# A selective scan and feed-forward block: four of sixteen u*B on ScalarE, C spread by transposes, ten C products on GpSimd

## The chip, the cores and the metric

The kernel runs on one core of a Trainium2 chip. A core has TensorE (matmuls), VectorE, ScalarE, GpSimd and SyncE (DMA queue); they run programs of their own and meet at semaphores. The metric is the device time of one execution, in microseconds.

## What is computed

The input is 16 sequences of 1024 tokens with 256 channels. First comes a selective scan with 16 states for each channel, then a normalisation, a gated feed-forward part with integer weights (hidden size 768), and a second normalisation.

```python
xz = einsum('btd,pd->btp', x, W_xproj)             # 64 rank, 16 B, 16 C
dt = softplus(einsum('btr,dr->btd', xz[..., :64], W_dt) + b_dt)
dA = exp(dt[..., None] * -exp(A_log))              # decay, per channel and state
dBx = dt[..., None] * B[:, :, None, :] * x[..., None]
h = dA_t * h + dBx_t;  y = sum_s h[..., s] * C[..., s]   # for each token
z = layernorm(x + y + Dp * x)
out = layernorm(z + (silu(z @ gate.T) * (z @ up.T)) @ down.T)
```

## The kernel before

The 16384 tokens are cut into 32 chunks of T = 512; two chunks make a sequence (par 0 and 1). Channels lie on the 128 partitions in DH = 2 halves q, tokens along the free dimension. All arithmetic on these tiles is f32, but for the gate and up matmuls (f16 in two parts).

For each chunk and state s, in this order: ScalarE makes the decay `exp(dt * a)` of each half into PSUM, in the one buffer `p_da` (L490); GpSimd makes `ub` = u * B_s (L388), where `u` = dt * x (L381) and B_s was spread over the partitions by a DMA through DRAM (`b_bc`); VectorE scans each half (L620) into `h`, which has eight slots; a product with C_s follows, in place, by GpSimd for the states of `POOL_STATES` (L398, C spread by DMA as `c_bc`) and by VectorE for the others (L629). For the latter TensorE spreads C_s into `p_c` by one bf16 matmul with a selector (L792), on three bf16 parts of the rows of C that `rest` and `third_part` (L594, L599) and three casts on ScalarE (L464, L468, L469) make. TensorE turns the products back to tokens on partitions and sums them over the states in `p_y` (L807). In chunks with par 0 ScalarE copies the last column as `h_carry` (L485), which the scans of the next chunk start from.

The rest of a chunk runs beside the scans of the next two: transposes and projections of the chunk ahead (`x_transposed`, `project`, `project_dt`, softplus in three ScalarE passes with a table load, `dt_of` L604), the first normalisation of the chunk behind (`stats1`, `mean1`, `norm_inputs`, a `pow` and a product on GpSimd L405 and L408, `norm1` L501), `x1_high` and `x1_low` (L506, L653), six tiles of gate and up matmuls (L831), `tanh` (L510), `silu` (L659), `hidden` (L665), and for the chunk two behind the down matmuls (L842), `residual` (L672), `stats2` and `norm2` (L518).

Each engine's order is written out by a loop over the 16 slots of a step (`step`), each with two or three zones; in slot s VectorE scans state s. The table `AT` gives the slot and zone of every other job. Ordinary u*B are made four slots ahead (`UB_AHEAD`), decays one ahead (`DA_AHEAD`), C products one behind (`C_LAG`, `POOL_LAG`), the sums two or three behind (`SUM_LAG`). An engine that waits holds up all that stands behind in its program:

```python
def decay(c, s, par, q):
    wait(act, s_dt, c + 1)
    wait(act, s_scan, 2 * units(c, s) - 2 + q - 1)   # scan of half q of the state before
def scan(c, s, par, batch, q):
    wait(dve, s_da, 2 * units(c, s) - 1 + q)
    if q == 0:
        wait(dve, s_ub, units(c, s))
```

Steps 0 and 1 are written out, a hardware loop runs pairs of steps, and the last steps are written out again; steps 32 and 33 hold only the normalisations and the feed-forward part of the last chunks.

Of the kernel before, what the change touches and what calls it, by code (L numbers as in the profile page):

```python
# [5 lines left out]
P = 128  # L6
# [7 lines left out]
T = 512  # L14
# [5 lines left out]
POOL_STATES = (1, 2, 4, 8, 9, 10, 11, 12)  # L20
# [7 lines left out]
SUM_LAG = {True: 3, False: 2}  # L28
# [19 lines left out]
B_GROUP = 4  # L48
UB_SLOTS = 8
# [3 lines left out]
def mamba_ffn_block(nc, x, w_xproj, w_dt, b_dt, a_log, d_skip, w_gate, w_up, w_down, out):  # L53
# [13 lines left out]

    assert N % B_GROUP == N % UB_SLOTS == N % H_SLOTS == 0

# [7 lines left out]
    with ExitStack() as ctx:  # L77
# [11 lines left out]
        selector = sb("selector", [P, N, P], BF16)  # L89
# [7 lines left out]
        wt_proj = sb("wt_proj", [P, DH, P], F32)  # L97
# [91 lines left out]
        s_b = [sem(f"s_b{k}") for k in range(N // B_GROUP)]  # L189
# [94 lines left out]
        def _(sp):  # L284
# [19 lines left out]
            def store(c):  # L304
                wait(sp, s_out_ready, c + 2)
# [30 lines left out]
            for k in range(N // B_GROUP):  # L336
# [27 lines left out]
        def _(pool):  # L364

            nc.gpsimd.memset(ident[:, :], 0.0).then_inc(s_fill, 1)
            nc.gpsimd.memset(selector[:, :, :], 0.0).then_inc(s_fill, 1)
            nc.gpsimd.memset(neg_half[:, :, :], -0.5)
            pool.wait_ge(s_fill, 2)
# [537 lines left out]
```

## Time and profile before

| | |
|---|---|
| median of 3 runs | 2120.16 us (2118.89 to 2121.01) |
| profiled execution, its time | 2119.75 us |
| its span, first to last instruction | 2118.0 us |
| mean granted TensorE clock | 0.928 of full |
| VectorE, GpSimd busy | 94%, 91% |
| TensorE, ScalarE busy | 74%, 62% |
| DMA | 239.9 MB, 113 GB/s |

PE stands for matmuls on TensorE, PEld for its weight loads, DVE for VectorE, ACT for ScalarE, POOL for GpSimd. A line such as L620 is a line of the kernel. Busy time is an average over the whole span, so the repeated part, the start and the tail have to be read apart.

### The profile page before, as it was taken

The numbers are of one execution on the slowest core, as the hardware profiler recorded it, in microseconds if no ns is written. First come the engines' busy times: TensorE is split into PE (matmuls) and PEld (weight loads), VectorE is DVE, ScalarE is ACT, GpSimd is POOL, SyncE is SP. The second block draws the span as 40 slices with busy tenths as digits, with TensorE's granted clock in tenths as the row PEclk, the third lists the DMA queues.
The fourth block names the chain that finished last, engine by engine and source line by source line (L and its number), as shares of the span: only waits on it lengthen the run. The fifth ranks groups of instructions, "written<-read, shape, count | busy, mean of one in ns | idle before, by whom it ended". The sixth has DMA issues, their size and how long they took to land.

```text
span 2118.0 us, 30230 instructions
## 1 busy us (share of the span) xinstructions
PE 1558.5 (74%) x8621; PEld 1140.7 (54%) x8744; DVE 1985.9 (94%) x2443; ACT 1303.6 (62%) x2157; POOL 1926.8 (91%) x877
## 2 busy tenths in 40 slices
PE   4677778777778777777777777777777877777775
PEld 1545555455555555555555555555555555555553
DVE  5799999999999999999999999999999999999982
ACT  4566666566666656666666666656666656666442
POOL 6999999999999999999999999999999999999950
PEclk6789999999999999999999999999999999999997
DMA  6332433223433322443322443422443422343200
GB/s 219 111 119 86 141 118 137 102 91 112 140 135 120 117 83 104 140 140 115 125 90 89 140 140 115 140 90 76 138 140 115 140 92 86 126 140 107 79 11 20
DMA packets 93455, 239.90 MB, mean 113 GB/s; under 512 B 8593, under 2 KB 42994, under 8 KB 77042
## 3 DMA queue, kind: packets, MB, share of 16 engines
q1 hardware_dynamic: 93426, 239.55, 32.5%
q8 instruction: 13, 0.21, 0.0%
q14 instruction: 16, 0.13, 0.0%
HBM read 220.65 MB, written 18.87 MB: 113 GB/s over the span
## 4 chain that ended last, share of the span: by engine, by line
issue 30%; POOL 28%; DVE 26%; PE 8%; ACT 6%; DVEq 2%; POOLq 1%; another core or an unknown queue 0%; ACTq 0%
POOL ub L388 16%; DVE h L620 10%; POOL h L398 8%; DVE h L629 6%; PE p_y L807 3%; DVE hid L665 2%; DVE silu_g L659 2%; ACT p_da L490 2%; DVE stats L635 2%; PE p_m L831 2%; DVEq L224 1%; PE p_o L842 1%; PE p_m L821 1%; POOL rstd L405 1%; DVE mean_var L639 1%
## 5 line engine op out<-in xcount | busy, mean ns | idle before, releaser
L388 POOL TENSOR_TENSOR ub<-u,b_bc 128x1024 f32<-128x1024 f32 x512 | 1203.9, 2372 | 0.1
L490 ACT ACTIVATE p_da<-dt,neg_a 128x512 f32<-128x512 f32 x1024 | 697.2, 687 | 426.1 <-DVE h L620 422.0
L620 DVE TENSOR_TENSOR_SCAN h<-p_da,h_carry,ub 128x512 f32<-128x512 f32 x512 | 641.5, 1271 | 2.2 <-ACT p_da L490 0.6
L398 POOL TENSOR_TENSOR h<-h,c_bc 128x1024 f32<-128x1024 f32 x256 | 606.8, 2371 | 33.5 <-ACT h_carry L485 32.8
L620 DVE TENSOR_TENSOR_SCAN h<-p_da,ub 128x512 f32<-128x512 f32 x512 | 610.1, 1212 | 8.1 <-ACT p_da L490 6.4
L807 PE MATMUL p_y<-ident,h 128*128 128x128 f32 x4096 | 572.2, 293 | 60.8 <-POOL h L398 59.6
L807 PEld LDWEIGHTS p_y<-ident,h 128*128 128x128 f32 x4096 | 518.8, 152 | 121.6 <-POOL h L398 81.9
L842 PE MATMUL p_o<-wt_down,hid 128*128 128x256 f32 x1536 | 353.7, 380 | 4.1 <-DVE hid L665 1.8
L842 PEld LDWEIGHTS p_o<-wt_down,hid 128*128 128x128 f32 x1536 | 287.6, 191 | 55.3 <-issue 13.9
L629 DVE TENSOR_TENSOR h<-h,p_c 128x1024 f32<-128x1024 f32 x256 | 306.1, 1196 | 9.8 <-PE p_c L792 5.2
L510 ACT ACTIVATE tanh_g<-p_m 128x512 f32<-128x512 f32 x192 | 114.7, 597 | 263.4 <-PE p_m L831 263.4
L831 PE MATMUL p_m<-x_t,wt_up 128*128 128x512 f16 x768 | 199.5, 382 | 80.5 <-DVE hid L665 78.6
L792 PE MATMUL p_c<-bc_parts,selector 128*128 128x512 bf16 x133 | 58.8, 442 | 268.4 <-DVE h L629 268.4
L831 PE MATMUL p_m<-x_t,wt_gate 128*128 128x512 f16 x768 | 199.7, 383 | 61.6 <-DVE x_t L653 55.1
L792 PEld LDWEIGHTS p_c<-bc_parts,selector 128*128 128x128 bf16 x256 | 26.8, 105 | 310.9 <-DVE h L629 208.4
L831 PEld LDWEIGHTS p_m<-x_t,wt_up 128*128 128x128 f16 x768 | 63.9, 98 | 207.7 <-DVE hid L665 149.9
L405 POOL TENSOR_TENSOR rstd<-var_eps,neg_half 128x8 f32<-128x8 f32 x33 | 54.0, 1638 | 130.3 <-DVE neg_mean L649 130.3
L659 DVE SCALAR_TENSOR_TENSOR silu_g<-tanh_g,p_m 128x512 f32<-128x512 f32 x192 | 127.9, 666 | 8.8 <-ACT tanh_g L510 8.8
L831 PEld LDWEIGHTS p_m<-x_t,wt_gate 128*128 128x128 f16 x768 | 64.4, 98 | 131.8 <-DVE x_t L653 62.8
L665 DVE SCALAR_TENSOR_TENSOR hid<-p_m,silu_g 128x512 f32<-128x512 f32 x192 | 128.1, 667 | 1.2 <-DVE silu_g L659 0.5
L381 POOL TENSOR_TENSOR u<-dt,x_t 128x1024 f32<-128x1024 f32 x32 | 76.4, 2388 | 18.1 <-DVE dt L604 18.1
L785 PE MATMUL p_m<-rank_t,wt_dt 65*128 65x512 f32 x128 | 67.9, 656 | 29.3 <-DVE bc_parts L599 29.3
(72 smaller groups left out, 1289.3 us busy)
## 6 DMA issues: line engine op xcount, KB each, us to landing
b_bc<-bc_rows_dram SPq DMA_DIRECT2D x128, 1024.0 KB, 4.7
c_bc<-bc_rows_dram SPq DMA_DIRECT2D x256, 256.0 KB, 6.5
x_in<-in_L_attn_x SPq DMA_DIRECT2D x32, 512.0 KB, 7.2
out_x<-res_n SPq DMA_DIRECT2D x32, 512.0 KB, 3.3
bc_rows_dram<-bc_rows SPq DMA_DIRECT2D x32, 64.0 KB, 2.3
hid<-in_L_ffn_w_gate SPq DMA_DIRECT2D x1, 768.0 KB, 4.9
hid<-in_L_ffn_w_up SPq DMA_DIRECT2D x1, 768.0 KB, 6.7
res<-in_L_ffn_w_down SPq DMA_DIRECT2D x1, 384.0 KB, 7.1
```

Source lines behind the costliest of these rows:

```text
L388: nc.gpsimd.tensor_tensor(ub[:, s % UB_SLOTS, :, :], u[:, par, :, :], b_bc[:, s:s + 1, :].broadcast_to([P, DH, T]), ALU.mult).then_inc(s_u ...
L398: nc.gpsimd.tensor_tensor(h[:, s % H_SLOTS, :, :], h[:, s % H_SLOTS, :, :], c_bc[:, i:i + 1, :].broadcast_to([P, DH, T]), ALU.mult).then_i ...
L490: nc.scalar.activation(p_da[:, q, :], dt[:, par, q, :], ACT.Exp, scale=neg_a[:, q, s:s + 1]).then_inc(s_da, 1)
L510: nc.scalar.activation(tanh_g[:, :], p_m[:, 0, :], ACT.Tanh, scale=0.5 / (QUANT * X1_SCALE)).then_inc(s_tanh, 1)
L620: nc.vector.tensor_tensor_scan(h[:, s % H_SLOTS, q, :], p_da[:, q, :], ub[:, s % UB_SLOTS, q, :], initial, ALU.mult, ALU.add).then_inc(s_s ...
L629: nc.vector.tensor_tensor(h[:, s % H_SLOTS, :, :], h[:, s % H_SLOTS, :, :], p_c[:, :, :].broadcast_to([P, DH, T]), ALU.mult).then_inc(s_hc ...
L659: nc.vector.scalar_tensor_tensor(silu_g[:, :], tanh_g[:, :], 1.0, p_m[:, 0, :], ALU.add, ALU.mult).then_inc(s_silu, 1)
L665: nc.vector.scalar_tensor_tensor(hid[:, j, :], p_m[:, 1, :], 1.0 / (2.0 * QUANT * QUANT * X1_SCALE * X1_SCALE), silu_g[:, :], ALU.mult, AL ...
L792: nc.tensor.matmul(p_c[:, 0, :], selector[:, s, :], bc_parts[:, par, :], start=True, stop=True).then_inc(s_c_ps, 1)
L807: ins = nc.tensor.matmul(p_y_tok[:, k, q * P:(q + 1) * P], h[:, s % H_SLOTS, q, k * P:(k + 1) * P], ident[:, :], start=False, stop=(s == S ...
L831: ins = nc.tensor.matmul(p_m[:, a, :], w[:, n % DH, j * P:(j + 1) * P], x1_t[:, n // DH, n % DH, :], start=(n == 0), stop=(n == 2 * DH - 1))
L842: ins = nc.tensor.matmul(p_o[:, k % 2, :], hid[:, j, k * P:(k + 1) * P], wt_down[:, j, :], start=(j == 0), stop=(j == NH - 1))
```

## The change

Four states, 3, 7, 11 and 15, get their u*B in another way. TensorE turns `u` to tokens on partitions (`u_transposed`, ScalarE copies it into `u_t`), and the rows of B and C too (`bc_turned`, `bc_cols` into `bc_t`). There B of a token is one number for a partition, so that ScalarE makes u*B by four passes of 128x256 with a scale (`times_b`, two slots ahead), and TensorE turns the result into `p_da` by eight transposes (`ub_transposed`). The decay of these states goes to SBUF, into two slots of `da_k`. GpSimd makes the other twelve.

C for VectorE's products is spread by four transposes of a column of `bc_t`, read with stride zero. The selector, `rest`, `third_part`, `second_parts` and the three casts go. GpSimd makes ten products with C instead of eight, VectorE six. `ub` has six slots instead of eight, b_bc twelve rows, and the sums lag by three and four slots. The table `AT` is new in most places. `wait` became `wait_ge` where the value is always positive, which issues the same.

```diff
-POOL_STATES = (1, 2, 4, 8, 9, 10, 11, 12)
+POOL_STATES = (0, 1, 2, 3, 4, 7, 8, 9, 10, 11)
-SUM_LAG = {True: 3, False: 2}
+SUM_LAG = {True: 4, False: 3}
...
-    "x_transposed": (0, 0), "x_out": (0, 1), "project": (1, 0), "rank_out": (1, 1), "bc_out": (1, 1), "rest": (2, 1),
-    "second_parts": (2, 0), "third_part": (2, 2), "project_dt": (2, 0), "softplus_abs": (4, 0), "softplus_exp": (4, 0), "softplus_log": (4, 0),
-    "dt_of": (4, 2), "u_of": (9, 0),
-    "z_out": (3, 0), "stats1": (3, 2), "mean1": (4, 0), "norm_inputs": (6, 1), "scalars": (7, 0), "norm1": (7, 0),
-    "x1_transposed": (8, 0), "x1_high": (8, 1), "x1_low": (9, 0),
-    "gate_up": (9, 2), "tanh": (9, 0), "silu": (10, 0), "hidden": (10, 1),
+    "x_transposed": (2, 1), "x_out": (2, 1), "project": (3, 0), "rank_out": (4, 1), "bc_out": (4, 1),
+    "project_dt": (4, 1), "softplus_abs": (5, 1), "softplus_exp": (6, 0), "softplus_log": (6, 1),
+    "dt_of": (7, 1), "u_of": (7, 1),
+    "u_transposed0": (12, 1), "u_out0": (15, 0), "u_transposed1": (15, 0), "u_out1": (15, 1),
+    "z_out": (4, 0), "stats1": (4, 2), "mean1": (5, 1), "norm_inputs": (7, 0), "scalars": (5, 0), "norm1": (7, 0),
+    "x1_transposed": (7, 2), "x1_high": (8, 0), "x1_low": (9, 0),
+    "gate_up": (9, 1), "tanh": (9, 0), "silu": (10, 0), "hidden": (10, 1),
...
-    "residual0": (3, 2), "residual1": (5, 1), "stats2": (5, 1), "mean2": (5, 2), "norm2": (14, 1),
+    "residual0": (2, 2), "residual1": (6, 0), "stats2": (6, 0), "mean2": (6, 1), "norm2": (10, 1),
+    "bc_turned": (7, 1), "bc_cols": (9, 1),
...
-B_GROUP = 4
-UB_SLOTS = 8
+K_STATES = (3, 7, 11, 15)
+K_AHEAD = 2
+K_SLOTS = 2
+GROUP = 4
+UB_SLOTS = 6
...
             def decay(c, s, par, q):
-                wait(act, s_dt, c + 1)
-                wait(act, s_scan, 2 * units(c, s) - 2 + q - 1)
-                nc.scalar.activation(p_da[:, q, :], dt[:, par, q, :], ACT.Exp,
-                                     scale=neg_a[:, q, s:s + 1]).then_inc(s_da, 1)
+                act.wait_ge(s_dt, c + 1)
+                if s in K_STATES:
+                    i = K_STATES.index(s)
+                    if i >= K_SLOTS:
+                        wait(act, s_scan, 2 * units(c, K_STATES[i - K_SLOTS]))
+                    else:
+                        wait(act, s_scan, 2 * units(c - 1, K_STATES[i - K_SLOTS + NK]))
+                    da = da_k[:, i % K_SLOTS, q, :]
+                else:
+                    wait(act, s_scan, 2 * units(c, s) - 2 + q - 1)
+                    da = p_da[:, q, :]
+                nc.scalar.activation(da, dt[:, par, q, :], ACT.Exp, scale=neg_a[:, q, s:s + 1]).then_inc(s_da, 1)
...
+            def times_b(c, s, par, half):
+                i = K_STATES.index(s)
+                if half == 0:
+                    act.wait_ge(s_bt, c + 1)
+                    act.wait_ge(s_ut, 2 * (c + 1))
+                    wait(act, s_ub_ps, DH * (k_units(c, s) - K_SLOTS))
+                for k in range(2 * half, 2 * half + 2):
+                    nc.scalar.activation(ub_t[:, i % K_SLOTS, k, :], u_t[:, k, :], ACT.Identity,
+                                         scale=bc_t[:, par, k, s:s + 1]).then_inc(s_ubt, 1)
...
+            def ub_transposed(c, s, q):
+                i = K_STATES.index(s)
+                pe.wait_ge(s_ubt, TT * k_units(c, s))
+                wait(pe, s_scan, 2 * units(c, s) - 2 + q - 1)
+                for k in range(TT):
+                    ins = nc.tensor.transpose(p_da[:, q, k * P:(k + 1) * P],
+                                              ub_t[:, i % K_SLOTS, k, q * P:(q + 1) * P], ident[:, :])
+                ins.then_inc(s_ub_ps, 1)
...
             def broadcast_c(c, s, par):
                 i = DVE_STATES.index(s)
-                wait(pe, s_parts, c + 1)
+                pe.wait_ge(s_bt, c + 1)
                 wait(pe, s_hc_dve, ND * c + i)
-                nc.tensor.matmul(p_c[:, 0, :], selector[:, s, :], bc_parts[:, par, :],
-                                 start=True, stop=True).then_inc(s_c_ps, 1)
+                for k in range(TT):
+                    ins = nc.tensor.transpose(p_c[:, 0, k * P:(k + 1) * P],
+                                              bc_t[:, par, k, N + s:N + s + 1].broadcast_to([P, P]), ident[:, :])
+                ins.then_inc(s_c_ps, 1)
...
+                        if zone == 0 and core and s in K_STATES:
+                            ub_transposed(c, s, 1)
...
+                        if zone == 2 and core and s + 1 in K_STATES:
+                            ub_transposed(c, s + 1, 0)
```

## Rows read from the trace of the kernel before

**Rows 1.** The page, busy us, share of the span and instructions of each engine.
```profile
PE 1558.5 (74%) x8621; PEld 1140.7 (54%) x8744; DVE 1985.9 (94%) x2443; ACT 1303.6 (62%) x2157; POOL 1926.8 (91%) x877
```
**Rows 2.** Windows, chunks 1 to 30: us; busy PE PEld DVE ACT POOL; PEclk; DMA.
```profile
93.48:1989.30 1895.82, 1428.60 (x8010) 1049.26 (x8128) 1845.35 (x2272) 1212.29 (x2006) 1799.59 (x813) 0.94 0.33 116
```
**Rows 3.** Groups by line on VectorE: busy us, mean ns, idle before, releaser.
```profile
L620 DVE TENSOR_TENSOR_SCAN h<-p_da,h_carry,ub 128x512 f32<-128x512 f32 x512 | 641.5, 1271 | 2.2 <-ACT p_da L490 0.6
L620 DVE TENSOR_TENSOR_SCAN h<-p_da,ub 128x512 f32<-128x512 f32 x512 | 610.1, 1212 | 8.1 <-ACT p_da L490 6.4
...
L604 DVE SCALAR_TENSOR_TENSOR dt<-p_m,dt 128x1024 f32<-128x1024 f32 x32 | 39.2, 1225 | 44.2 <-ACT dt L481 44.2
```
**Rows 4.** Timeline of VectorE, slots 1 and 2 of one chunk: start us, us, engine, line, operation.
```profile
922.08 1.20 DVE L629 TENSOR_TENSOR h<-h,p_c 128x1024 f32<-128x1024 f32 x1
923.19 1.22 DVE L620 TENSOR_TENSOR_SCAN h<-p_da,ub 128x512 f32<-128x512 f32 x1
924.44 0.71 DVE L594 TENSOR_TENSOR p_m<-p_m,bc_parts 64x512 f32<-64x512 f32 x1
925.18 1.22 DVE L620 TENSOR_TENSOR_SCAN h<-p_da,ub 128x512 f32<-128x512 f32 x1
926.44 0.68 DVE L599 TENSOR_TENSOR bc_parts<-p_m,bc_mid 32x512 bf16<-32x512 f32 x1
927.15 2.34 DVE L620 TENSOR_TENSOR_SCAN h<-p_da,ub 128x512 f32<-128x512 f32 x2
```
**Rows 5.** Timeline of VectorE, `third_part`, first scans of chunks 1 and 31, end of 31.
```profile
17.32 0.69 DVE L599 TENSOR_TENSOR bc_parts<-p_m,bc_mid 32x512 bf16<-32x512 f32 x1 [1.25 <-ACT bc_parts L469]
...
93.48 2.45 DVE L620 TENSOR_TENSOR_SCAN h<-p_da,h_carry,ub 128x512 f32<-128x512 f32 x2
...
1989.30 2.45 DVE L620 TENSOR_TENSOR_SCAN h<-p_da,h_carry,ub 128x512 f32<-128x512 f32 x2
...
2050.60 1.19 DVE L629 TENSOR_TENSOR h<-h,p_c 128x1024 f32<-128x1024 f32 x1
```
**Rows 6.** Timeline of GpSimd, the start and one run of u*B.
```profile
27.77 2.98 POOL L381 TENSOR_TENSOR u<-dt,x_t 128x1024 f32<-128x1024 f32 x1 [18.07 <-DVE dt L604]
...
975.36 11.65 POOL L388 TENSOR_TENSOR ub<-u,b_bc 128x1024 f32<-128x1024 f32 x5
...
1006.31 1.64 POOL L405 TENSOR_TENSOR rstd<-var_eps,neg_half 128x8 f32<-128x8 f32 x1 [3.08 <-DVE neg_mean L649]
```
**Rows 7.** Groups by line on ScalarE.
```profile
L490 ACT ACTIVATE p_da<-dt,neg_a 128x512 f32<-128x512 f32 x1024 | 697.2, 687 | 426.1 <-DVE h L620 422.0
...
L481 ACT ACT_TABLE_LOAD x32 | 41.1, 1283 | 0.6
...
L477 ACT ACTIVATE dt<-dt 128x1024 f32<-128x1024 f32 x32 | 33.9, 1058 | 1.0
...
L458 ACT COPY rank_t<-p_m 64x512 f32<-64x512 f32 x32 | 18.6, 580 | 16.4 <-PE p_m L777 16.4
```
**Rows 8.** Timeline of ScalarE, the first row copy and one `norm1`.
```profile
14.20 0.58 ACT L463 COPY bc_rows<-p_m 32x512 f32<-32x512 f32 x1
...
1008.35 2.08 ACT L501 ACTIVATE x<-z,shift,rstd 128x256 f32<-128x256 f32 x4 [0.21 <-POOL shift L408]
```
**Rows 9.** Timeline of TensorE: a gap, then transposes at the low and the high clock.
```profile
945.59 0.61 PE L792 MATMUL p_c<-bc_parts,selector 128*128 128x512 bf16 x1 [5.47 <-DVE h L629]
945.99 3.62 PE L807 MATMUL p_y<-ident,h 128*128 128x128 f32 x16
949.69 1.04 PE L821 MATMUL p_m<-ident,x 128*128 128x128 f32 x8
950.57 1.04 PE L807 MATMUL p_y<-ident,h 128*128 128x128 f32 x8
```
**Rows 10.** Windows on TensorE: us, busy (instructions), granted clock, DMA share, GB/s.
```profile
946.00:949.60 3.60, 3.60 (x17) 0.51 0.29 107
949.60:951.60 2.00, 1.91 (x17) 1.00 0.96 394
```

More of the change, by code:

```diff
@@ L66, in mamba_ffn_block @@
     DVE_STATES = [s for s in range(N) if s not in POOL_STATES]
-    assert N % B_GROUP == N % UB_SLOTS == N % H_SLOTS == 0
+    NK = len(K_STATES)
+    B_STATES = [s for s in range(N) if s not in K_STATES]
+    NB = N - NK
+    B_GROUP = NB // NK
+    assert K_STATES == tuple(range(GROUP - 1, N, GROUP)) and B_GROUP == GROUP - 1
+    assert NB % UB_SLOTS == N % H_SLOTS == NK % K_SLOTS == 0
     sum_at = {s: s + SUM_LAG[s in POOL_STATES] for s in range(N)}
@@ L120, in mamba_ffn_block @@
         h = sb("h", [P, H_SLOTS, DH, T], F32)
+        u_t = sb("u_t", [P, TT, D], F32)
+        ub_t = sb("ub_t", [P, K_SLOTS, TT, D], F32)
+        da_k = sb("da_k", [P, K_SLOTS, DH, T], F32)
         h_carry = sb("h_carry", [P, N, DH], F32)
@@ L188, in mamba_ffn_block @@
         s_rows_dram = sem("s_rows_dram")
-        s_b = [sem(f"s_b{k}") for k in range(N // B_GROUP)]
+        s_b = [sem(f"s_b{k}") for k in range(N // GROUP)]
+        s_ut_ps = sem("s_ut_ps")
+        s_ut = sem("s_ut")
+        s_ubt = sem("s_ubt")
+        s_ub_ps = sem("s_ub_ps")
         s_ub = sem("s_ub")
@@ L335, in _ @@
             rows_out(0, 0)
-            for k in range(N // B_GROUP):
+            for k in range(N // GROUP):
                 broadcast_b(0, k, 0)
@@ L366, in _ @@
             nc.gpsimd.memset(ident[:, :], 0.0).then_inc(s_fill, 1)
[L367 removed]
             nc.gpsimd.memset(neg_half[:, :, :], -0.5)
[L369 removed]
+            pool.wait_ge(s_fill, 1)
             nc.gpsimd.affine_select(out=ident[:, :], in_=ident[:, :], compare_op=ALU.not_equal, fill=1.0,
                                     base=0, pattern=[[-1, P]], channel_multiplier=1).then_inc(s_const, 1)
[L373 to L377 removed]
             def u_of(c, par):
[L380 removed]
+                pool.wait_ge(s_dt, c + 1)
                 nc.gpsimd.tensor_tensor(u[:, par, :, :], dt[:, par, :, :], x_t[:, par, :, :],
@@ L532, in _ @@
                 decay(0, 0, 0, q)
+            bc_cols(0, 0)
+            for a in range(2):
+                u_out(0, a)
             act.wait_ge(s_const, 1)
@@ L548, in step @@
                         if nxt and due("bc_out"):
-                            bc_out(c + 1, 1 - par)
-                        if nxt and due("second_parts"):
-                            second_parts(c + 1, 1 - par)
+                            bc_out(c + 1)
+                        if nxt and due("bc_cols"):
+                            bc_cols(c + 1, 1 - par)
+                        for a in range(2):
+                            if nxt and due(f"u_out{a}"):
+                                u_out(c + 1, a)
+                        ck, sk, pk = unit_at(c, s, K_AHEAD, par)
+                        if core and (sk >= K_AHEAD or nxt) and sk in K_STATES:
+                            times_b(ck, sk, pk, zone)
                         if nxt and due("softplus_abs"):
@@ L674, in residual @@
                     x1[:, 2 * a:2 * a + 2, :], ALU.mult, ALU.add).then_inc(s_res, 1)
-            rest(0, 0)
-            third_part(0, 0)
             dt_of(0, 0)
@@ L690, in step @@
                                     residual(c - 2, a)
-                        if nxt and due("rest"):
-                            rest(c + 1, 1 - par)
-                        if nxt and due("third_part"):
-                            third_part(c + 1, 1 - par)
                         if prev and due("stats1"):
@@ L834, in gate_up, with down @@
                     ins.then_inc(done, 1)
-            def down(c, k, half):
+            def down(c, k, half, turned):
                 if k == 0 and half == 0:
-                    wait(pe, s_hid, NH * (c + 1))
+                    pe.wait_ge(s_hid, NH * (c + 1))
+                    wait(pe, s_bt, turned)
+                    wait(pe, s_ut, 2 * turned)
                 if k % 2 == 0 and half == 0:
@@ L847, in _ @@
             x_transposed(0)
-            pe.wait_ge(s_wt, 3)
+            pe.wait_ge(s_wt, 2)
             project(0, 0)
@@ L851, in _ @@
             project_dt(0)
-            pe.wait_ge(s_const, 4)
+            bc_turned(0)
+            for a in range(2):
+                u_transposed(0, 0, a)
             pe.wait_ge(s_skip_diag, 2)
@@ L872, in step @@
                             project_dt(c + 1)
+                        if nxt and due("bc_turned"):
+                            bc_turned(c + 1)
+                        for a in range(2):
+                            if nxt and due(f"u_transposed{a}"):
+                                u_transposed(c + 1, 1 - par, a)
                         if prev and due("x1_transposed"):
```

204 lines of the change are left out of this document (109 added, 95 removed), and 4 rows, old and new, of the table AT.

## The prediction

> **What bounds the kernel now.** I read the busy times first: VectorE 94%, GpSimd 91%, TensorE 74%, ScalarE 62% [rows 1]. Then the stretch between the first scans of chunks 1 and 31, which leaves out start and tail: 30 chunks in 1895.82 us, 63.19 each, of which VectorE is busy 61.5, GpSimd 60.0, TensorE 47.6 and ScalarE 40.4 [rows 2]. So VectorE is the bound with 1.7 us of idle a chunk, GpSimd is 1.5 us behind it, and ScalarE mostly waits for VectorE (422 us behind scans [rows 7]). The reader should see that no engine can be relieved alone. Of the 1.7 us idle, 44.2/32 = 1.4 are one wait: the `dt` sum (L604) for the softplus chain [rows 3]. Around the repeated part stand 93.48 us of start, which holds chunk 0 [rows 5], 62.5 us of chunk 31 (1989.30 to about 2051.8) and 66.2 us of tail, in which latency rules. The profiled span is 2118.0, the execution 2119.75, the median of the runs 2120.16: I add 1.75 to the span.
>
> "Slot s" is the piece of each engine's program in which VectorE scans state s.
>
> **What goes, VectorE.** Two products with C (8 to 6): start to start one costs 923.19 - 922.08 = 1.11 us, so 2.22. The pass for `rest`: 0.74 (924.44 to 925.18), and its scan takes 1.25 instead of 1.12 to the next start, 0.13 more; `third_part` and its scan the same, 0.71 + 0.14 [rows 4]. Together 1.72. VectorE loses 3.94 us a chunk: 63.19 - 3.94 = 59.25 with all waits left as they are. The softplus steps are now spread over slots 5 and 6 and the `dt` sum stands in slot 7, behind residual, statistics and a product: its wait of 1.4 goes, 57.87 is left. The eight scans of the four ScalarE states have their operands swapped (decay in SBUF, u*B in PSUM). No row shows that; each scan before has one operand in each memory too, and its two forms differ by 0.06 us [rows 3]. I take 0, and 8 x 0.06 = 0.5 either way as the bound.
>
> **GpSimd.** Twelve u*B instead of sixteen, ten products with C instead of eight: two fewer, at 11.65/5 = 2.33 us [rows 6], 60.0 - 4.66 = 55.3. It stays below 57.87, by 2.5 us: no bound, but a short lead. Its queue now meets the norm's `pow` in slot 5, while VectorE makes the inputs in slot 7; that wait re-anchors GpSimd once a chunk.
>
> **ScalarE.** Added: 16 passes of 128x256 at 0.52 (four chained took 2.08 [rows 8]), 8.3 us; two copies of u, 512 columns each from PSUM, 2 x 0.58 (as L458); one copy of B and C columns, 128 elements, no more than the 0.58 of 512, for which I take 0.3 [rows 7]. Removed: three casts of 512 columns, again 0.58 each, 1.7. So 40.4 + 8.0 = 48.4 of some 59. The total fits; the order is what matters, because there is one PSUM buffer for the decay and ordinary decays must follow the scans closely. The four decays into `da_k` may run ahead, which gives ScalarE room in each slot before 3, 7, 11, 15. Their destination is SBUF: 0.69 into PSUM, and 1.06 for twice the size within SBUF [rows 7], so 0.53 to 0.69; hidden either way.
>
> **TensorE.** Added 32 transposes of u*B, 8 of u, 4 of the B/C rows and 24 for C, 68 in all; eight take 950.57 - 949.69 = 0.88 us, so 7.5 us, less eight bf16 matmuls of 0.2. From 47.6 to about 53.5 busy: no bound by itself. At the low clock eight take 1.81 (sixteen in 3.62) [rows 9]. What is new is that a scan waits for it: in a ScalarE state four transposes (0.44 at the full clock, 0.91 at the low one, plus 1.04 - 0.88 = 0.16 to the end of the last, and the hand-over) must fit within the 1.12 us in which the other half is scanned.
>
> **DMAs.** B in rows of three states instead of four and two more rows of C: 22 rows instead of 24. Broadcasts for groups are issued as GpSimd frees them, 10 us and more ahead of use: nothing. The row write itself goes from slot 1 to slot 4, still 20 us ahead of the first use (GpSimd's u*B for state 0 about 30 us after slot 7 begins). The store and the load before them on SyncE's queue have as much.
>
> **The walk over the slots.** With t=0 where VectorE makes the norm inputs (slot 7), a scan pair 2.3, a C product 1.11, `silu` and `hidden` 0.58 each, the slots begin at 8: 4.7, 9: 7.0, 10: 10.4, 11: 13.9, 12: 17.3, 13: 20.8, 14: 25.4, 15: 30.0, 0: 34.6, 1: 38.0, 2: 40.3, 3: 43.2, 4: 45.5, 5: 49.1, 6: 51.7, 7: 57.4. GpSimd, from t = 2.1 (`pow` 1.64 and `shift`), at 2.33 each: u*B 9 done at 4.4, C of 4 at 6.8, u*B 10 at 9.1, u 11.4, u*B 12 at 13.8, C 7 at 16.1, u*B 13 at 18.4, C 8, u*B 14 at 23.1, C 9, C 10, u*B 0 at 30.1, C 11, u*B 1 at 34.7, and the last, C 3, at 55.7. Each u*B is there 1.9 us or more before its scan. New waits that I find on VectorE:
> - Slot 8: norm inputs, `pow` to 2.1, ScalarE's four passes to 4.2, the decay behind them to 4.85; the scan could start at 4.7. About 0.35 with hand-overs.
> - Slot 10: ScalarE's `tanh` (512 columns from PSUM, 0.6 like L458) waits for the first gate matmuls, then come the B/C copy, half of a u*B (1.04) and the decay: 0.35.
> - Slot 11: `norm2` (2.06) stands between two decays: 0.5.
> - Slot 1: two halves of u*B (2.08) around the decay, with a carry copy in even chunks: 0.1.
> - Transposes that come late: 0.2.
>
> Sum 1.5, so the period is 57.87 + 1.5 = 59.4.
>
> **Start and tail.** `project_dt` waited for `third_part`, which ended at 18.0 [rows 5]; now for the row copy, which ended at 14.8 [rows 8]: 3.2 us earlier. Chunk 0 runs on GpSimd's queue: from 27.77 - 3.2 = 24.5 [rows 6], 3.0 for u and 23 operations of 2.33 to u*B 0 of chunk 1 make 81; ScalarE's weight copies and softplus may push the first scan of chunk 1 to 87. I take 84, where it was 93.5. Chunk 31: 62.5 less two products (2.2) and the odd wait, 59.5. The tail keeps its 66.2, its order is the same. Together 209.7, and 30 x 59.4 = 1782: span 1991.7, time **1993 us**.
>
> **TensorE's clock, rule against row.** The clock falls now once a chunk, behind its longest gap: 5.5 us before 945.59 [rows 9], then 0.51 granted over 946.0 to 949.6, the level of 1.2 GHz. It rises again though TensorE did almost nothing but transposes in between: 1.00 right behind [rows 10]. After the change the emptiest part (slots 5 to 8) holds transposes for states 7 and C 5 and 6, so that its longest gap is some 2.9 us: I count the clock as full, and a low stretch as part of the range (late gate matmuls, about 2.7 us in slot 10: 0.9 for each of two sums with eight transposes, and 0.9 for the gate).
>
> The Trainium skill ("TensorE: Matmul & The Clock Gate", Part 4: PE-mode transpose) says that transposes do not count as activity for the clock gate. By that, slots 5 to 9 would run at the low clock whatever the change puts there, the period would be 59.4 + 2.7 = 62.1 and the time near 2074. This trace speaks against it: behind nothing but transposes the granted clock is 1.00. I count it with the first rival, at 0.06 of that case's chance.
>
> **The rivals.**
> 1. *ScalarE cannot keep up* in order. If running ahead in the `da_k` states does not help, what it has per slot (with 1.28 for a table load and 1.06 for a softplus pass [rows 7]) counts against VectorE's slot: slot 1 3.5 against 2.3, slot 5 (2.08 + `Abs` 1.0 + decays 1.3) 4.4 against 2.7, slot 6 (two softplus passes, two table loads, two decays) 6.0 against 5.7, slot 9 4.5 against 3.4, with slots 8 and 11 0.9: 5.2 us. Period 57.87 + 5.2 = 63.1, time 2104. For it: one decay buffer and 422 us of ScalarE bound to scans now. Against it: slots 4, 6 and 7 of VectorE are long just there. A low clock in slots 5 to 9 gives 62.1 and 2074 without it, so that this case, with either cause, is 2029 to 2112.
> 2. *Slower: TensorE's queue stands between the engines.* A sum of a GpSimd state (C 4, C 7, C 9 end 1.2 to 1.9 us behind their slots in the walk above) stops TensorE, and behind it wait the gate matmuls (on which ScalarE's `tanh` and then the next decay hang) and the transposes for states 7 and 15. Price: 2.7 in slot 10, and twice 1.9 + 0.9 (the sum) + 0.7 (the transposes) - 1.1 of cover = 2.4; with the waits above 9.0. Period 66.9, time 209.7 + 2007 + 1.75 = 2218. It decides from (2118.0 - 209.7)/30 = 63.6, that is from 5.7 us of new waits a chunk.
> 3. *No change:* new waits of 5.6 to 5.8 us a chunk eat the gain, a period near 63.6. It would take the first two together at just that size.
>
> **How the numbers follow.** Forecast case, period 58.2 to 60.6, 1957 to 2029: 0.62. First rival: 0.24. Slower: 0.10. Within 0.2% (about what a measurement of this kernel can tell from no change): 0.02. Faster than 1957, GpSimd's 55.3 and VectorE's 57.87 hardly allow: 0.02. The range leaves out the upper half of the first rival and everything slower: 1957 to 2080. Faster 0.88, same 0.02, slower 0.10.
>
> **What would show it.** Right: first scans of chunks 59 to 60 us apart; VectorE's idle before the `dt` sum gone; busy sums a chunk near 57.5, 55.3, 53.5, 48.4; ScalarE's passes with no scan waiting on them for over 0.5. Wrong: idle of the scans put down to ScalarE's decay (first rival) or to TensorE's transposes and `tanh` (second), a granted clock near 0.5 in slots 5 to 9, or the scans of the four states slower than 1.27.

## The result and the profile after

The changed kernel takes **2038.49 us** (2036.85 to 2039.64) where the kernel before takes 2120.47 on the same chip: ratio 0.9614 (95% interval 0.9603 to 0.9626), 82 us less. The forecast was 1993, 127 less. The time lies inside the range, but in the band 2029 to 2112 of the first rival and not in that of the forecast case.

Lines of the page of the kernel after: engines, the four passes of u*B, the decays into SBUF, the scans of the four ScalarE states (two forms).

```profile
PE 1723.9 (85%) x10664; PEld 1333.4 (66%) x10664; DVE 1874.8 (92%) x2315; ACT 1475.1 (72%) x2668; POOL 1770.1 (87%) x809
...
L528 ACT ACTIVATE ub_t<-u_t,bc_t 128x256 f32<-128x256 f32 x512 | 230.1, 497 | 0.4
L514 ACT ACTIVATE da_k<-dt,neg_a 128x512 f32<-128x512 f32 x256 | 179.8, 717 | 0.4
L662 DVE TENSOR_TENSOR_SCAN h<-da_k,p_da 128x512 f32<-128x512 f32 x128 | 155.4, 1215 | 15.9 <-PE p_da L840 11.1
...
L662 DVE TENSOR_TENSOR_SCAN h<-da_k,h_carry,p_da 128x512 f32<-128x512 f32 x128 | 162.2, 1274 | 4.4 <-PE p_da L840 4.1
```

The stretch between the first scans of chunks 1 and 31, by windows (us, then busy PE, PEld, DVE, ACT, POOL, granted clock, DMA share and GB/s); it answers to [rows 2].

```profile
82.91:1909.37 1826.46, 1589.49 (x9927) 1234.64 (x9925) 1742.22 (x2151) 1373.41 (x2486) 1658.81 (x752) 0.96 0.34 113
```

The span went from 2118.0 to 2035.1. Of the 82.9, 10.6 came in the start (93.48 to 82.91), 3.0 in chunk 31 and the tail (128.7 to 125.7), and 69.4 in the 30 chunks. Start and end are as forecast (82.91 + 125.7 = 208.6, forecast 209.7). **The whole miss is in the period: 1826.46/30 = 60.88 us, forecast 59.4.**

A chunk's busy sums are VectorE 58.1, GpSimd 55.3, TensorE 53.0, ScalarE 45.8 (forecast 57.5, 55.3, 53.5, 48.4). So the engines' work was counted well, and the idle of VectorE was not: 60.88 - 58.07 = 2.8 a chunk. The waits of VectorE in that stretch show where (us in total, times, longest), first before, then after.

```profile
DVE dt L604 <- ACT dt L481: 31.9, 30, 2.3
DVE h L620 <- ACT p_da L490: 7.0, 16, 0.6
DVE h L629 <- PE p_c L792: 2.7, 1, 2.7
DVE x_t L653 <- ACT x_t L506: 2.7, 12, 0.2
```

```profile
DVE silu_g L700 <- ACT tanh_g L548: 32.3, 24, 2.0
DVE h L670 <- PE p_c L849: 20.1, 30, 1.8
DVE h L662 <- PE p_da L840: 12.6, 28, 0.6
DVE h L662 <- ACT p_da L514: 12.3, 30, 0.7
```

The wait for the softplus chain is gone. In its place stand `silu` behind `tanh` in slot 10 (1.08 a chunk), the product with C of state 5 behind its transposes in slot 6 (0.67), the scans of ScalarE states behind their transposes (0.42), and decays in slot 8 (0.41).

**The wait in slot 10.** TensorE, GpSimd and VectorE of the kernel after, by timeline (start, us, engine, line, operation, idle before it and who ended it):

```profile
1024.42 1.09 PE L886 MATMUL p_m<-ident,x 128*128 128x128 f32 x8 [2.38 <-ACT x L539]
1026.74 3.46 PE L872 MATMUL p_y<-ident,h 128*128 128x128 f32 x16 [1.23 <-POOL h L411]
1030.00 1.25 PE L896 MATMUL p_m<-x_t,wt_gate 128*128 128x512 f16 x4
```

```profile
1020.15 1.64 POOL L418 TENSOR_TENSOR rstd<-var_eps,neg_half 128x8 f32<-128x8 f32 x1 [5.88 <-DVE neg_mean L690]
...
1024.34 2.35 POOL L411 TENSOR_TENSOR h<-h,c_bc 128x1024 f32<-128x1024 f32 x1
```

```profile
1027.38 1.20 DVE L694 SCALAR_TENSOR_TENSOR x_t<-p_m,x_t 128x1024 f16<-128x1024 f32 x1
...
1031.91 0.69 DVE L700 SCALAR_TENSOR_TENSOR silu_g<-tanh_g,p_m 128x512 f32<-128x512 f32 x1 [1.08 <-ACT tanh_g L548]
```

GpSimd stands 5.88 us in front of `pow`, and only behind it makes the product with C 4, until 1026.7. TensorE's sum of state 4 waits for that product, and the gate matmuls stand behind the sum in TensorE's queue. They need only `x1_low`, which ended at 1028.58, but start at 1030.00. The sixteen transposes of the sum take 3.46 us because the granted clock over them is 0.55. At the full clock sixteen would take some 1.8 (an estimate, twice the 0.88 from start to start of eight in [rows 9]), and the gates would start with the end of `x1_low`. So two things meet here, a late product and a low clock; experiments 1 and 2 take them apart.

**The wait in slot 6.** By windows TensorE works without a gap for 26 us, from the transposes for C 15 at 995.76 to 1022.

```profile
996.00:1015.00 19.00, 19.00 (x106) 15.64 (x105) 18.35 (x27) 14.34 (x29) 18.27 (x8) 1.00 0.18 61
1015.00:1020.00 5.00, 5.00 (x48) 5.00 (x47) 4.12 (x11) 4.97 (x7) 0.00 (x0) 1.00 0.99 278
```

At its end its queue is late, and VectorE's product waits for what stands there (VectorE by timeline):

```profile
1018.69 1.22 DVE L670 TENSOR_TENSOR h<-h,p_c 128x1024 f32<-128x1024 f32 x1 [0.88 <-PE p_c L849]
```

### The profile page after: what moved, and what is told of

Its sections match the earlier page's. It is cut to its first block, busy times and chain, and to the rows that moved or that the text cites. A ratio compares the mean times of both kernels' runs of the same rounds, so it can differ in the third digit from the quotient of the medians.

```text
span 2035.1 us, 35587 instructions
## 1 busy us (share of the span) xinstructions
PE 1723.9 (85%) x10664; PEld 1333.4 (66%) x10664; DVE 1874.8 (92%) x2315; ACT 1475.1 (72%) x2668; POOL 1770.1 (87%) x809
## 4 chain that ended last, share of the span: by engine, by line
PE 49%; issue 15%; ACT 14%; DVE 14%; POOL 6%; DVEq 1%; ACTq 0%; POOLq 0%; SPq 0%; DMA 0%
PE p_o L909 16%; PE p_y L872 13%; PE p_m L896 7%; POOL h L411 4%; DVE h L670 4%; DVE h L662 3%; DVE hid L706 3%; ACT p_da L514 3%; PE p_c L849 3%; PE p_m L820 3%; PE p_m L812 3%; ACT da_k L514 3%; ACT res_n L556 2%; PE p_da L840 2%; DVE silu_g L700 2%
## 5 line engine op out<-in xcount | busy, mean ns | idle before, releaser
L401 POOL TENSOR_TENSOR ub<-u,b_bc 128x1024 f32<-128x1024 f32 x384 | 905.8, 2373 | 0.1
L411 POOL TENSOR_TENSOR h<-h,c_bc 128x1024 f32<-128x1024 f32 x320 | 755.2, 2371 | 0.0
L514 ACT ACTIVATE p_da<-dt,neg_a 128x512 f32<-128x512 f32 x768 | 524.4, 686 | 231.7 <-DVE h L662 229.6
L662 DVE TENSOR_TENSOR_SCAN h<-p_da,h_carry,ub 128x512 f32<-128x512 f32 x384 | 474.6, 1266 | 8.8 <-ACT p_da L514 8.0
L662 DVE TENSOR_TENSOR_SCAN h<-p_da,ub 128x512 f32<-128x512 f32 x384 | 452.4, 1208 | 9.8 <-ACT p_da L514 9.1
L528 ACT ACTIVATE ub_t<-u_t,bc_t 128x256 f32<-128x256 f32 x512 | 230.1, 497 | 0.4
L514 ACT ACTIVATE da_k<-dt,neg_a 128x512 f32<-128x512 f32 x256 | 179.8, 717 | 0.4
L662 DVE TENSOR_TENSOR_SCAN h<-da_k,p_da 128x512 f32<-128x512 f32 x128 | 155.4, 1215 | 15.9 <-PE p_da L840 11.1
L662 DVE TENSOR_TENSOR_SCAN h<-da_k,h_carry,p_da 128x512 f32<-128x512 f32 x128 | 162.2, 1274 | 4.4 <-PE p_da L840 4.1
L840 PE MATMUL p_da<-ident,ub_t 128*128 128x128 f32 x1024 | 139.5, 274 | 10.6 <-DVE h L662 10.6
```

The costliest lines, as they stand in the source:

```text
L401: nc.gpsimd.tensor_tensor(ub[:, i % UB_SLOTS, :, :], u[:, par, :, :], b_bc[:, i:i + 1, :].broadcast_to([P, DH, T]), ALU.mult).then_inc(s_u ...
L411: nc.gpsimd.tensor_tensor(h[:, s % H_SLOTS, :, :], h[:, s % H_SLOTS, :, :], c_bc[:, i:i + 1, :].broadcast_to([P, DH, T]), ALU.mult).then_i ...
L514: nc.scalar.activation(da, dt[:, par, q, :], ACT.Exp, scale=neg_a[:, q, s:s + 1]).then_inc(s_da, 1)
L528: nc.scalar.activation(ub_t[:, i % K_SLOTS, k, :], u_t[:, k, :], ACT.Identity, scale=bc_t[:, par, k, s:s + 1]).then_inc(s_ubt, 1)
L662: nc.vector.tensor_tensor_scan(h[:, s % H_SLOTS, q, :], da, dbx, initial, ALU.mult, ALU.add).then_inc(s_scan, 1)
L840: ins = nc.tensor.transpose(p_da[:, q, k * P:(k + 1) * P], ub_t[:, i % K_SLOTS, k, q * P:(q + 1) * P], ident[:, :])
```

## The experiments

My theory after the result: both new waits are TensorE's, one by GpSimd's late product in front of the gate matmuls, one by its long full run. The rivals: ScalarE's passes; the low clock; or that eight products would have been the better split.

### 1. `pow` one slot later

```diff
-"norm_inputs": (7, 0), "scalars": (5, 0),
+"norm_inputs": (7, 0), "scalars": (6, 0),
```

> The changed kernel with one entry of the table moved: the norm's pow and product on GpSimd ("scalars") from slot 5 to slot 6, so that u*B of state 9 and C of state 4 run ahead of its wait, in the 5.9 us that GpSimd idles there. Theory TensorE (the sum of state 4 holds TensorE's queue for GpSimd, the clock falls behind that gap, the first gate matmuls and with them tanh and silu come late): VectorE's wait before silu, 32.3 us over 30 chunks, goes; the time falls by 25 to 35 us from 2038.5, ratio to the kernel before 0.944 to 0.950, and no granted clock below 1.00 is left in slots 8 and 9. Rival ScalarE (its order makes tanh late, behind a u*B half and the decays): time within 4 us of 2038.5.

Measured: 2000.74 us, ratio 0.9431 (0.9416 to 0.9447), 37.7 under the changed kernel, a little more than the 35 expected at most; period 59.67. VectorE's waits now:

```profile
DVE h L670 <- PE p_c L849: 20.1, 30, 1.8
DVE h L662 <- PE p_da L840: 12.6, 28, 0.6
DVE h L662 <- ACT p_da L514: 12.3, 30, 0.7
...
DVE silu_g L700 <- ACT tanh_g L548: 0.4, 2, 0.2
```

Only the first wait has gone, from 32.3 us to 0.4, and the gaps between chunks, irregular before (59.4 to 62.0), are 59.0 and 60.0 in turn. GpSimd makes C 4 ahead of `pow`, and waits for it 2.46 us instead of 5.88. The low clock, though, is still there in some chunks: over the sixteen transposes of this sum the granted clock is 1.00 in 17 of the 30 chunks and 0.52 to 0.73 in the other 13. Windows of this kernel, in one of the 13:

```profile
1009.00:1011.80 2.80, 0.42 (x4) 0.18 (x3) 2.68 (x3) 2.80 (x7) 2.72 (x4) 1.00 0.02 7
...
1012.90:1016.10 3.20, 3.20 (x17) 3.20 (x17) 3.20 (x4) 2.98 (x8) 3.20 (x2) 0.52 0.80 310
1016.10:1018.00 1.90, 1.90 (x12) 0.99 (x11) 1.90 (x2) 1.20 (x4) 1.90 (x2) 1.00 0.00 0
```

Here the sixteen transposes take 3.41 us, nearly all of them at 0.52 granted, and the gates start at 1016.14, just behind the end of `x1_low` at 1015.97: the low clock lies in time that TensorE has. The expectation that no clock below 1.00 would be left was a miss. With the product early, the low clock costs next to nothing; what the late product costs without it, experiment 2 shows.

### 2. Transposes for C 5 made three times, 0.88 us more on TensorE in the full run

```diff
-                for k in range(TT):
+                for k in list(range(TT)) * (3 if s == 5 else 1):
```

> The changed kernel with the four transposes of C for state 5 made three times, same result: 0.88 us more of TensorE a chunk, just ahead of VectorE's product for state 5. Theory TensorE (its queue is full from slot 0 to 7 and the product waits for it): the wait before the products grows from 20.1 us over 30 chunks by up to 0.88 x 30 = 26, the time by 18 to 28 us, to about 2061. Rival (the wait has another cause, TensorE has room): less than 5 us.

Measured: 2054.73 us, ratio 0.9692 (0.9676 to 0.9708), 16.2 over the changed kernel, just under the 18 to 28 expected. The wait for `p_c` grows by 26.2 us, the whole 0.88 a chunk; 6 of it come back at `silu`:

```profile
DVE h L670 <- PE p_c L849: 46.3, 30, 2.7
DVE silu_g L700 <- ACT tanh_g L548: 26.1, 16, 2.1
```

So work in the full run is paid in full, by the next wait at least.

What came back at `silu` came by the clock. GpSimd's product C 4 is equally late in all 30 chunks of this kernel: the sum behind it starts 2.42 to 2.52 us after the start of `x1_transposed`. The granted clock over its sixteen transposes is 0.50 (the level of 1.2 GHz) in 16 chunks, 1.00 in eight and 0.78 in six, and the whole 26.1 us of `silu` waits lie in the 16. A chunk of the first kind, then one of the second (clock 0.50 over 1036.20 to 1039.90, 1.00 over 1097.90 to 1100.00), TensorE and VectorE by timeline:

```profile
1036.24 3.67 PE L872 MATMUL p_y<-ident,h 128*128 128x128 f32 x16 [0.47 <-POOL h L411]
1039.71 1.44 PE L896 MATMUL p_m<-x_t,wt_gate 128*128 128x512 f16 x4
...
1097.95 1.97 PE L872 MATMUL p_y<-ident,h 128*128 128x128 f32 x16 [1.34 <-POOL h L411]
1100.06 1.04 PE L896 MATMUL p_m<-x_t,wt_gate 128*128 128x512 f16 x4
```

```profile
1041.81 0.69 DVE L700 SCALAR_TENSOR_TENSOR silu_g<-tanh_g,p_m 128x512 f32<-128x512 f32 x1 [1.48 <-ACT tanh_g L548]
...
1102.28 0.66 DVE L700 SCALAR_TENSOR_TENSOR silu_g<-tanh_g,p_m 128x512 f32<-128x512 f32 x1
```

The kernel after shows the same split: 24 chunks at 0.50 to 0.57 hold all but 0.1 of the 32.3 us (0.68 to 1.97 each), six at 0.74 to 0.79 hold that 0.1, with the sum late by 2.2 to 2.5 in both groups. So the wait needs both, the late product and the low clock. Either one alone costs almost nothing.

### 3. ScalarE's passes over 128 of 256 columns

Left out: u*B of half the channels in the four ScalarE states; those stay zero.

```diff
-nc.scalar.activation(ub_t[:, i % K_SLOTS, k, :], u_t[:, k, :], ...
+nc.scalar.activation(ub_t[:, i % K_SLOTS, k, 0:P], u_t[:, k, 0:P], ...
```

> The changed kernel with the 16 ScalarE passes of u*B made over 128 instead of 256 columns; the other half of the channels is left out for these four states (it is zero). ScalarE has some 16 x 0.13 = 2 to 3 us less a chunk, nothing else changes. Theory TensorE: the waits before silu, the C product of state 5 and the scans of state 3 stay, time 0 to 8 us under 2038.5. Rival ScalarE: the waits shrink by 1 us a chunk or more, 30 us or more under.

Measured: 2030.3 us, ratio 0.9570 (0.9554 to 0.9586), 8.2 less, at the edge of the 0 to 8 expected. ScalarE has 1.6 us less a chunk (1324.13 busy in 30 chunks instead of 1373.41) and the period falls by 0.26, of it most at `silu` (25.3 us instead of 32.3). The passes are a fifth shorter (391 ns instead of 497), and 8.2 of the 45 us of the miss come back: ScalarE's order, the first rival of the prediction, isn't its main cause.

### 4. Eight products with C on GpSimd, the rest of the change kept

```diff
-POOL_STATES = (0, 1, 2, 3, 4, 7, 8, 9, 10, 11)
+POOL_STATES = (0, 1, 2, 3, 4, 8, 9, 10)
```

> The changed kernel with GpSimd's products with C taken back from ten to eight (states 7 and 11 to VectorE, C for them spread by eight more transposes of TensorE). The prediction counts a product at 1.11 us of VectorE: 2 x 1.11 x 32 = 71 us over the changed kernel, to about 2109, if VectorE's time counts one for one; 35 to 50 us if the waits of the changed kernel (2.8 us a chunk) cover part of it, or if GpSimd's earlier products take the wait before silu away.

Measured: 2072.09 us, ratio 0.9772 (0.9756 to 0.9788), 33.6 more, just under the 35 to 50 expected. VectorE's busy time grows by 2.1 a chunk (1805.45/30 = 60.2), the period only by 1.19, to 62.07. The difference is the wait at `silu`, which was 32.3 us:

```profile
DVE silu_g L700 <- ACT tanh_g L548: 3.4, 5, 0.8
```

So the two products that went to GpSimd took 2.1 from VectorE, and 0.9 came back as the wait at `silu`. Not because C 4 is later with ten products: the sum behind it starts 2.2 to 2.6 after `x1_transposed` here too. But VectorE now has the product with C 7 ahead of `x1_low`, which ends 5.1 to 5.5 us after that start instead of 4.0 to 4.7, and the clock over the sum is 1.00 in 21 of 30 chunks; the 3.4 us lie in the five at 0.50. Experiment 1 removes the wait without giving up the products.

### 5. Moving the late transposes forward within the full run

The kernel of experiment 1 with C 5 put first in slot 5 (a), and with the transposes for state 3 also earlier, in slot 2 (b).

```diff
+                        if zone == 0 and core and s == 5:
+                            broadcast_c(c, 5, par)
...
+                        if zone == 1 and core and s == 2:
+                            ub_transposed(c, 3, 0)
...
-                            ub_transposed(c, s + 1, 0)
+                            ub_transposed(c, s + 1, 1 if s == 2 else 0)
```

> e1 with the four transposes of C for state 5 issued one slot earlier on TensorE, ahead of the sum of state 1. Theory TensorE (the wait of 20.1 us over 30 chunks before VectorE's product is the queue ahead of these transposes): that wait goes, 12 to 20 us under e1's 2000.7, to 1981 to 1989. Rival (the slots are full, another piece of TensorE's queue becomes late instead, as in e4): 0 to 5 us under e1.

> e6 with the transposes of u*B of state 3 issued earlier on TensorE: the first half ahead of the transposes of x, the second ahead of the sum of state 15. Theory TensorE: the waits before the scans with u*B in PSUM (12.6 us over 30 chunks, state 3 alone) go, 8 to 13 us under e6. Rival (x, the projection and the down matmuls then come 0.4 us later in a full queue): no change against e6, within 4 us.

Measured: 2000.92 (ratio 0.9437, 0.9421 to 0.9452) and 2000.15 (0.9431, 0.9415 to 0.9446) against 2000.74 in experiment 1: nothing. The waits of (a), then of (b):

```profile
DVE h L662 <- PE p_da L840: 29.9, 57, 0.7
DVE h L662 <- ACT p_da L514: 12.3, 30, 0.7
DVE h L662 <- ACT da_k L514: 3.2, 15, 0.5
DVE h L670 <- PE p_c L849: 2.6, 1, 2.6
```

```profile
DVE h L662 <- ACT da_k L514: 33.3, 45, 2.0
DVE h L662 <- ACT p_da L514: 12.3, 30, 0.7
```

The wait for `p_c` goes and as much comes elsewhere: (a) at the scans behind transposes that now stand later, (b) at decays, since `x`'s transposes and with them ScalarE's `x_out` come later (in one chunk of (b) ScalarE stands 1.61 us for those transposes at 991.71, and VectorE's scan 1.15 for the decay behind `x_out`). In this run without a gap the order chooses only who waits.

### 6. The full run started earlier, or made shorter

The kernel of experiment 1 with the first two down products put into slot 0 ahead of the transposes for C 15 (TensorE used to stand there, for a product of VectorE's):

```diff
+                            if last and s == 0:
+                                for i in range(2):
+                                    down(c - 2, 0, i, c + 1 if core else CHUNKS)
...
-                            for i in range(2 * TT):
+                            for i in range(2, 2 * TT):
```

> e1 with the first two halves of the down matmuls moved ahead of the transposes of C for state 15, into the 1.4 us in which TensorE stands still before them at the start of each chunk; no work is added or taken. Theory full queue (from there to slot 7 TensorE works 24 us without a gap, and this run's length, not the place of any one job in it, sets the waits of VectorE before the C product of state 5 and the scans of states 3 and 7, which is why e6 and e7 gained nothing): the run starts 1.3 us earlier, those waits (1.2 us a chunk) go, 22 to 36 us under e1's 2000.7. Rival (the period of 59.7 is set by a loop through GpSimd and ScalarE and the waits only show its slack): within 5 us of e1.

Measured: **1961.38 us**, ratio 0.9248 (0.9233 to 0.9264), 39.4 under experiment 1 (expected 22 to 36) and the fastest here that makes the whole computation. Period 58.45, 1.22 less. The row of the kernel after that it removes, then the waits of this kernel:

```profile
995.76 0.65 PE L849 MATMUL p_c<-ident,bc_t 128*128 128x128 f32 x4 [1.57 <-DVE h L670]
```

```profile
DVE h L662 <- ACT p_da L514: 14.2, 30, 0.8
DVE h L670 <- PE p_c L849: 5.6, 16, 1.8
```

No work was taken away. The run uses the 1.57 us in which TensorE had stood, and the period gives back 1.22. The other way, with less work: experiment 1 with a third of the hidden channels left out of the down products.

```diff
-                for j in range(3 * half, 3 * half + 3):
+                for j in (3 * half, 3 * half + 2):
```

> e1 with two of each three down matmuls (a third of the hidden units is left out of the down projection): TensorE has eight matmuls of 0.22, 1.8 us, less a chunk, all in its full stretch. In the tail alone this gives some 10 us (e8 against the kernel before: 118.9 instead of 128.7 from the first scan of chunk 31 to the end). Theory full queue: the repeated part gives another 25 to 36 us, the first scans of chunks 58.6 us apart instead of 59.7, about 1957. Rival loop: only the tail's 10 us.

Measured: 1952.22 us, ratio 0.9210 (0.9195 to 0.9225); TensorE has 2.4 us less a chunk (1477.18 busy in 30 chunks, 1549.10 in experiment 1). The period is 58.35, 1.32 under experiment 1 and a little more than the 1.1 expected, with 7.4 less in the last chunk and tail (116.5 against 123.9) and 2.6 in the start. It is nearly the period of the early start, reached by another way: with either, TensorE's run no longer sets it. VectorE is then idle for 0.7 to 0.8 a chunk.

Both moves of experiment 5 on top of the early start:

> e11 with the transposes of C for state 5 and of u*B for state 3 issued earlier as in e6 and e7. Theory full queue: where e11 leaves some of these waits, they go now, 0 to 8 us under e11. Rival loop: as e1.

Measured: 1983.77 us, ratio 0.9358 (0.9342 to 0.9373), 22.4 over the early start alone. I had expected at best a small gain; it was a clear loss. Its waits:

```profile
DVE h L662 <- ACT da_k L514: 18.4, 44, 2.0
DVE h L662 <- ACT p_da L514: 12.3, 30, 0.7
DVE h L662 <- PE p_da L840: 6.0, 15, 0.4
```

I read it so: once the run isn't the bound, a bad place in it costs its own price.

### 7. The softplus spread in the kernel before

The prediction credits 1.4 us a chunk to this part alone. So it was made alone, in the kernel before, then with a third of the hidden channels left out of the down products (as above), with and without the spread.

```diff
-"softplus_exp": (4, 0), "softplus_log": (4, 0), "dt_of": (4, 2),
+"softplus_exp": (4, 1), "softplus_log": (5, 1), "dt_of": (6, 2),
```

> The kernel before with only its softplus spread out: exp from zone 0 to zone 1 of slot 4, the logarithm to slot 5, the dt sum from slot 4 to slot 6. If the 1.38 us wait for the softplus chain simply goes, as the prediction counted: 30 to 44 us under the kernel before, ratio 0.979 to 0.986. Rival (another wait takes its place, x1's transposes or GpSimd 1.5 us behind): ratio 0.993 to 1.000.

Measured: 2121.91 us, ratio 1.0005 (0.9996 to 1.0015): no difference. The wait at `dt` is gone. The waits are now:

```profile
DVE h L629 <- remote: 24.9, 30, 2.8
DVE p_m L594 <- ACT bc_parts L464: 11.5, 12, 1.1
```

"remote" stands for a releaser that the trace doesn't give. The waiting product is that of state 3, and by the timeline TensorE is at work without a gap from `project_dt` at 1060.60 to the selector matmul for the next product at 1073.07 (12.42 us busy of 12.47). I read it as the same thing as in experiment 5; to test that, TensorE got less work:

> The kernel before with two of each three down matmuls (a third of the hidden units is left out of the down projection), as a control for e9: TensorE has 16 x 2... in numbers 8 matmuls of 0.22 = 1.8 us less a chunk. VectorE waits for softplus as before. Both theories: 0 to 6 us under the kernel before, most of it in the tail.

> e8 with the softplus spread as in e4. Theory TensorE (in e4 the 1.4 us of the softplus wait came back as waits for C of state 3 and for the down matmuls, since TensorE works without a gap from project_dt to the last of them): with 1.8 us less in that stretch the gain appears, 30 to 44 us under e8. Rival GpSimd (its 60.0 us and its waits make a period near 63 and spreading softplus can't help): within 8 us of e8.

Measured: 2112.17 (0.9960, 0.9946 to 0.9974) without the spread and 2115.80 (0.9976, 0.9967 to 0.9986) with it. The expectation, 30 to 44 us between the two, fell. The ten executions of the second lie in two groups, four near 2111 us and six near 2117, and its trace is of one of the four (2111.66), so that it doesn't show what the six have more. The first one gains 7.7 us (expected 0 to 6), in the tail alone (118.9 against 128.7); its period is 63.31. The timeline of TensorE, and VectorE's product, in the second:

```profile
1117.62 1.96 PE L785 MATMUL p_m<-rank_t,wt_dt 65*128 65x512 f32 x4 [1.97 <-DVE bc_parts L599]
1119.42 3.50 PE L800 MATMUL p_y<-skip_diag,x_t 128*128 128x128 f32 x16
...
1125.44 0.38 PE L792 MATMUL p_c<-bc_parts,selector 128*128 128x512 bf16 x1
```

```profile
1125.85 1.22 DVE L629 TENSOR_TENSOR h<-h,p_c 128x1024 f32<-128x1024 f32 x1 [1.36 <-PE p_c L792]
```

With less work ahead of it TensorE stands 1.97 us before `project_dt`, and behind that the granted clock is 0.52: the sixteen matmuls take 3.50 instead of the 1.95 that they take in the spread kernel with all its work. The low clock took 1.6 back just where 1.8 had been saved (eight of 24 down matmuls, which take 5.40 from start to start in the spread kernel). So this run doesn't settle whether TensorE alone held the spread kernel; it shows only that a shorter run isn't always an earlier one. In chunks of the other parity this kernel gains (gaps of 61.9 where 62.4 to 63.0), in these it loses (64.4 where 63.6).

## Why the prediction was right and wrong

**Right.** The bound: VectorE, GpSimd close behind, and the sums for each engine within 0.6 us, but for ScalarE's, which was 2.6 too high. Of that 1.1 is its sixteen passes, 215.73 us in 30 chunks or 7.2 a chunk where the forecast had 8.3: two chained ones take 0.90 from start to end. The rest I haven't split. The swapped operands of the scans: 1215 and 1274 ns against 1212 and 1271 [rows 3], so the 0 of the forecast. The start, chunk 31 and the tail came in as forecast. The decay in slot 8: 0.35 forecast, 0.41 measured. GpSimd: 55.3 exactly.

**Wrong, in the period, 1.5 us.** It splits into three, all read between the first scans of chunks 1 and 31.

- *The removed wait, 0.3.* The step "1.4 are one wait" divided the 44.2 us of [rows 3] by 32 chunks. That row is of the whole span, and 12.3 us of it are two waits of the start; in the 30 chunks it is 31.9 us, 1.06 each.
- *New waits, 0.7.* The list came to 1.5, and with the 0.4 of old waits that stay (12.4 us in 30 chunks) to 1.9; measured were 2.6 (78 us in 30 chunks). Term by term: slot 8, 0.35 and 0.41. Slot 10, **0.35 and 1.08**. Slot 11, 0.5 and none. Slot 1, 0.1 and none. "Transposes that come late", **0.2 and 1.09** (0.67 for C 5, 0.42 for u*B).
- *VectorE's busy time, 0.5.* It fell by 3.4 and not by 3.9. Part of this is the waits again: an operation begins 0.09 before the end of the one ahead of it (1.11 from start to start, 1.20 long [rows 4]), but not behind a wait. The kernel with few waits (experiment 6) has 57.7 busy, the changed one 58.1.

**The steps that failed** are thus slot 10 and the transposes, the two terms that go through TensorE's queue, and for slot 10 also "I count the clock as full". Slot 10: the second rival of the prediction had this very mechanism (a sum for C 4 stops the queue, gate matmuls wait behind it) at 2.7, and gave it to the tenth that was slower. It came at 1.08 a chunk, because `x1_low` would have held the gates until 1028.6 anyway. In the walk, C of 4 was done at 6.8, in front of slot 9; I went on with VectorE from there, and not with what stands behind that sum in TensorE's queue. The wait that "re-anchors GpSimd once a chunk" was noted and its price not: it stood 5.5 us a chunk (165.3 in 30), all of it with C 4 behind it. Experiment 1 takes the whole term away and gains 37.7 us; some 10 of them (0.35 a chunk) were in the forecast, the others are more than half of the 45 that it missed.

The transposes: I compared TensorE's 53.5 us with the 59 of a chunk and found no bound. The mean hides that 26 of them lie in one run without a gap, at whose end the queue is late. Experiments 2, 5 and 6 show it: more work there costs, another order doesn't help, an earlier start gives 1.22 back.

**The time fell in the first rival's band.** That case had two causes, ScalarE's order or a low clock in slots 5 to 9. ScalarE's order is not the main one: experiment 3 finds 0.26 of a period in 1.6 us of ScalarE's work. The low clock is half of one. It came at the end of slot 8 and not from slot 5 on (1.00 from 996 to 1020), and the wait of 1.08 a chunk came only where it met the late product; the prediction had put 2.7 on it. The range goes up to 2080 for this rival's sake, so that it holds the measured time in part by luck: the case came in with other sizes than those it was priced by.

**The clock** was argued wrongly, and the whole wait of slot 10 hangs on it. I took 2.9 us for the longest gap and counted the clock as full, since [rows 9] showed it low behind 5.5. After the change it is low once a chunk behind 2.38 or less, 0.55 over the 3.5 us from 1026.7. With it at 1.00 the late product costs nothing (eight chunks of experiment 2), and with GpSimd early the low clock costs nothing (experiment 1).

**The term for the spread softplus** held in the changed kernel as far as its wait is gone; no run measures what it is worth there. Alone it is worth nothing in the kernel before (experiment 7). What is late next was the question, and I didn't ask it: there it is the product of state 3.

## What to carry to other kernels

Beside an engine's busy share, read its longest run without a gap and what starts it: there a job's place only chooses who waits, while starting the run earlier moves everything. Put an engine's wait for another behind the work that third engines need from it (one number in a table was 37.7 us here). Two jobs moved into a gap ahead of a full run were worth 39.4. Where a wait comes and goes from chunk to chunk, sort the chunks by clock before naming its cause: here it took a late product and a low clock together. Take a wait's size from the repeated stretch and not from a whole-span row, and before counting it as gained, find who is late next.

## What the hardware did that I had not expected

- **Less work, lower clock.** In experiment 7 TensorE had 2.75 us of down matmuls ahead of `project_dt` instead of 4.05, stood 1.97 us for it, and got 0.52 of its clock from 1119.4 to 1122.7. In the changed kernel the clock fell behind 2.38 us of idle, eight transposes and 1.23 more, and in experiment 1 behind 2.38 and the transposes alone, where [rows 9] had shown 5.47. The gap alone doesn't decide it: in experiment 1 TensorE stands 2.2 to 2.4 us ahead of `x1_transposed` in 29 of the 30 chunks, and over the sum behind it the clock is below 0.75 in 12 of them and 1.00 in 17. No run was made that varies the gap.
- **It rises behind transposes again.** In experiment 1 there is nothing but transposes from 1011.80 to 1016.1, and the granted clock right behind is 1.00. That doesn't agree with the Trainium skill ("TensorE: Matmul & The Clock Gate", Part 4: PE-mode transpose), by which transposes don't count as activity; by that rule the f16 gates would have begun low.
- ScalarE's decay in the kernel after is 686 ns long into PSUM and 717 into SBUF, for the same 512 columns. The Trainium skill ("ScalarE: Activation LUTs", Step-by-step: what each stage is for) calls PSUM the faster destination for ScalarE, which agrees.
